# Halving the expert's unit of work in a fused one-core block stack, and moving elementwise work between GpSimd, ScalarE and VectorE

## Time and profile before

| | |
|---|---|
| runs, median of 3 | 3956.78 us (3954.4 to 3968.36) |
| the profiled execution, its own time | 3952.47 us |
| its span, first to last instruction | 3950.7 us |
| mean granted TensorE clock | 0.878 |
| TensorE busy | 3197.8 us (81%) |
| GpSimd busy | 3007.5 us (76%) |
| VectorE busy | 2802.2 us (71%) |
| ScalarE busy | 2373.0 us (60%) |
| DMA | 710.42 MB, mean 180 GB/s |

### The profile page before, as it was taken

One profiled execution on the slowest core, in us unless ns is written; L12 is line 12 of the kernel. 1 busy time (PEld: TensorE's weight loads), 2 busy tenths in 40 slices (PEclk: granted clock), 3 DMA queues, 4 the chain that ended last, 5 costly groups with the idle time before them and its releaser, 6 DMA issues. The chain is left out here.

```text
span 3950.7 us, 58606 instructions
## 1 busy us (share of the span) xinstructions
PE 3197.8 (81%) x17648; PEld 1963.8 (50%) x17648; DVE 2802.2 (71%) x5886; ACT 2373.0 (60%) x5235; POOL 3007.5 (76%) x2719
## 2 busy tenths in 40 slices
PE   5878787898879988798977988799877988769327
PEld 3545354564536654365544645366543655436105
DVE  3357878776886778677687677866787777877760
ACT  5566666666666656565676656666575656644321
POOL 1128888877888679786888778886898878898980
PEclk9888798899889998899888998799988998889558
DMA  2036777767687677776777676876777767797970
GB/s 67 6 90 180 207 181 197 207 162 211 173 211 189 164 213 183 199 188 191 193 193 199 173 209 164 218 192 166 215 186 195 188 190 200 184 245 208 242 179 32
DMA packets 406459, 710.42 MB, mean 180 GB/s; under 512 B 52922, under 2 KB 86338, under 8 KB 406146
## 3 DMA queue, kind: packets, MB, share of 16 engines
q1 hardware_dynamic: 406146, 706.68, 67.1%
HBM read 622.63 MB, written 83.89 MB: 179 GB/s over the span
## 5 line engine op out<-in xcount | busy, mean ns | idle before, releaser
L1417 POOL TENSOR_TENSOR u_rows<-u_rows,c_rows 128x512 f32<-128x512 f32 x1024 | 1340.4, 1310 | 325.9 <-DVE state L1227 255.5
L1410 POOL TENSOR_TENSOR u_rows<-u_rows,b_rows 128x512 f32<-128x512 f32 x1024 | 1348.3, 1318 | 14.6 <-DMA u_rows<-u_dram 14.1
L907 ACT ACTIVATE bank<-d_rows,a_rep 128x512 f32<-128x512 f32 x1024 | 693.4, 685 | 345.4 <-DMA d_rows<-delta_dram 148.0
L1222 DVE TENSOR_TENSOR_SCAN u_rows<-bank,state,u_rows 128x512 f32<-128x512 f32 x512 | 642.0, 1270 | 108.3 <-ACT bank L907 64.7
L1222 DVE TENSOR_TENSOR_SCAN u_rows<-bank,u_rows 128x512 f32<-128x512 f32 x512 | 622.6, 1216 | 108.1 <-ACT bank L907 99.7
L629 PE MATMUL bank<-u_rows,sum_n 128*32 128x512 f32 x2048 | 329.0, 719 | 357.2 <-POOL u_rows L1417 357.0
L749 ACT ACTIVATE prob<-prob,neg_max 128x256 f32<-128x256 f32 x1024 | 508.3, 501 | 83.9 <-DVE neg_max L1013 83.7
L1013 DVE CUSTOM_DVE_ANT_0 prob<-bank,band 128x256 f32<-128x256 f32 x896 | 337.0, 417 | 177.5 <-PE bank L460 141.7
L472 PE MATMUL bank<-ident,prob 128*128 128x128 f32 x2048 | 344.2, 298 | 115.6 <-ACT prob L749 55.5
L472 PEld LDWEIGHTS bank<-ident,prob 128*128 128x128 f32 x2048 | 256.7, 152 | 265.0 <-issue 173.6
L460 PE MATMUL bank<-kT,q_own 32*128 32x256 f32 x2048 | 317.5, 429 | 36.4 <-DVE neg_max L1013 26.2
(11 more groups left out here) (161 smaller groups left out, 5715.3 us busy)
## 6 DMA issues: line engine op xcount, KB each, us to landing
u_rows<-u_dram SPq DMA_DIRECT2D x1024, 256.0 KB, 5.0
d_rows<-delta_dram SPq DMA_DIRECT2D x1024, 256.0 KB, 5.0
zs_dram<-region_b SPq DMA_DIRECT2D x64, 256.0 KB, 2.7
xc_dram<-region_b SPq DMA_DIRECT2D x64, 256.0 KB, 2.6
delta_dram<-region_b SPq DMA_DIRECT2D x64, 256.0 KB, 2.1
u_dram<-region_b SPq DMA_DIRECT2D x64, 256.0 KB, 2.0
yg<-xc_dram SPq DMA_DIRECT2D x64, 256.0 KB, 3.3
zg<-zs_dram SPq DMA_DIRECT2D x64, 256.0 KB, 4.0
```

Of the source, the lines that this page charges most:

```text
L907: e.activation(banks[at.bank][:, :], delta_of(i, k), ACT.Exp, scale=a_rep[:, j:j + 1]).then_inc(filled[at.bank], 1)
L1222: e.tensor_tensor_scan(rows, banks[at.bank][:, :], rows, state[:, k:k + 1] if i % 2 else 0.0, ALU.mult, ALU.add).then_inc(drained[at.bank], 1)
L1410: e.tensor_tensor(rows, rows, b_rows[:, :], ALU.mult).then_inc(bx_ready.sem, 1)
L1417: e.tensor_tensor(rows, rows, c_rows[:, :], ALU.mult).then_inc(hc_ready.sem, 1)
```

## The change

1. `expert` is made for each group instead of each pair: 25 steps, 2 parts of 256 rows, between 0.44 and 0.97 of every period (group i in period i+4). A new stage `fetch` (0.39 to 0.40) loads the weights; for the second group of a pair it loads the two large ones once more, except for the last two pairs, where no MLP needs `w_1` and `w_2` in between. The MLP's weights are loaded back after each expert that still has an MLP to come.
2. GpSimd no longer forms `diff`, the squares or the epsilon sums. ScalarE makes `(1-mu)*x_prev` (four copies with a scale, from two new constants `not_mu_k` and `not_mu_r`); VectorE adds `mu*x` to it, makes the squares and the epsilon sums.
3. In scans 14 and 15 VectorE makes the product with B for the odd tiles, reading B from its PSUM bank, which stays taken until the last of them; GpSimd keeps the even tiles and all products with C.

```diff
@@ costs and threads
-    "route": [1] * 4,
-    "expert": [1] * 49,
+    "route": [1] * 3,
+    "fetch": [1],
+    "expert": [1] * 25,
...
-    (("route",), 3, 0.36, 0.40),
-    (("expert",), 3, 0.44, 0.97),
+    (("route",), 3, 0.36, 0.39),
+    (("fetch",), 4, 0.39, 0.40),
+    (("expert",), 4, 0.44, 0.97),
...
+def shared_inputs(i, batches):
+
+    return i >= 2 * batches - 2
...
-        return ([("b", 0, 1), ("c", 7, 8)]
+        return ([("b", 0, SCAN0 + 2 * (TILES - 1) + INPUT_AT if shared else 1), ("c", 7, 8)]
...
+        def fetched_again(i):
+
+            return i % 2 and i - 1 < 2 * BATCH - 4
@@ pe_mlp
-            if i % 2 == 0 and i >= 4:
-                e.wait_ge(*w_back.at(i // 2 - 2, 2))
+            if i >= 4:
+                e.wait_ge(*w_back.at(i - 4, 2))
@@ act_rwkv
             act_transposed(e, (use("t3.0"), use("t3.1")), norm_b)
             yield
+            e.wait_ge(*gone(use("t3.0")))
+            e.wait_ge(*gone(use("t3.1")))
+            for a, mu in ((1, "not_mu_k"), (0, "not_mu_r")):
+                for k in range(KD):
+                    e.activation(mixT[:, a, k, :], nb[:, k, 0:G], ACT.Copy, scale=col[mu][:, k:k + 1]).then_inc(mix_half.sem, 1)
@@ dve_stats
             e.wait_ge(*ln.stat.at(i, 3 * k + 2))
+            e.tensor_scalar(ln.rstd[:, :], ln.mean_var[:, :, 1], EPS, None, ALU.add)
@@ dve_rwkv
-            e.wait_ge(*diff_ready.at(i))
             for a, mu in ((1, "mu_k"), (0, "mu_r")):
                 for k in range(KD):
-                    e.scalar_tensor_tensor(out=mixT[:, a, k, :], in0=diff[:, k, :], scalar=col[mu][:, k:k + 1],
-                                           in1=nb[:, k, 0:G], op0=ALU.mult, op1=ALU.add).then_inc(mix_ready.sem, 1)
+                    e.wait_ge(*mix_half.at(i, 2 * (1 - a) + k + 1))
+                    e.scalar_tensor_tensor(out=mixT[:, a, k, :], in0=nb[:, k, 1:1 + G], scalar=col[mu][:, k:k + 1],
+                                           in1=mixT[:, a, k, :], op0=ALU.mult, op1=ALU.add).then_inc(mix_ready.sem, 1)
...
-            yield from range(8)
+            yield
+            for m in range(KD):
+                e.wait_ge(*gone(use(f"rk{m}")))
+                e.tensor_tensor(kT2[:, m, :], kT2[:, m, :], kT2[:, m, :], ALU.mult).then_inc(k_sq.sem, 1)
...
@@ dve_scan
+            def times_b(k):
+                at, rows = use("b"), rows_of(i, k)
...
+                e.wait_ge(*landed(u_landed, i * TILES + k))
+                ins = e.tensor_tensor(rows, rows, banks[at.bank][:, :], ALU.mult)
+                ins.then_inc(bx_by_vector.sem, 1)
...
             for step in range(SCAN_STEPS):
+                k = tile_at(step, INPUT_AT)
+                if k is not None and k % 2 and shared_inputs(i, BATCH):
+                    times_b(k)
@@ pool_rstd
-            e.tensor_scalar(ln.rstd[:, :], ln.mean_var[:, :, 1], EPS, None, ALU.add).then_inc(ln.power.sem, 1)
@@ pool_rwkv
-            e.tensor_tensor(diff, nb[:, :, 1:1 + G], nb[:, :, 0:G], ALU.subtract).then_inc(diff_ready.sem, 1)
...
-                e.tensor_tensor(kT2[:, m, :], kT2[:, m, :], kT2[:, m, :], ALU.mult).then_inc(k_sq.sem, 1)
@@ sp_fetch
+            if i % 2 == 0 or fetched_again(i):
+                e.wait_ge(*pick_ready.at(i // 2))
+                pick = e.value_load(top_i[0:1, 0:1], min_val=0, max_val=EXPERTS - 1)
+                e.wait_ge(*full(uses["mlp", min(i + 3, 2 * BATCH - 1), "m3"]))
+                if i:
+                    e.wait_ge(*gone(uses["expert", i - 1, "e1.5"]))
```

More of the change, by code:

```diff
@@ L132, in __init__, with banks_of @@
         self.bank, self.n, self.f = bank, n, f
[L135 removed]
+def banks_of(order, batches):
     begins, ends = {}, {}
     for stage in COSTS:
[L139 to L141 removed]
+        for shared in (False, True):
+            for name, first, last in uses_of(stage, shared):
+                begins.setdefault((stage, shared, first), []).append(name)
+                ends.setdefault((stage, shared, last), []).append(name)
     idle, counted, signalled, uses = list(range(8)), [0] * 8, [0] * 8, {}
     for stage, i, step in order:
[L144 removed]
+        shared = stage == "scan" and shared_inputs(i, batches)
+        for name in begins.get((stage, shared, step), ()):
             bank = idle.pop(0)
@@ L148, in banks_of @@
             signalled[bank] += not (stage == "scan" and name[0] == "y")
-        for name in ends.get((stage, step), ()):
+        for name in ends.get((stage, shared, step), ()):
             idle.append(uses[stage, i, name].bank)
```

188 lines of the change are left out of this document (96 added, 92 removed).

## The result

The changed kernel takes 3789.24 us, the median of 4 runs (3782.69 to 3797.62); the kernel before took 3957.41 in the same sessions (4 runs). The ratio is 0.9571, 95% interval 0.9544 to 0.9599: 168 us faster, where the forecast said 103. The profiled execution took 3792.8 us, its span is 3790.9, the mean granted clock 0.911 (0.878 before).

What follows compares the result with a forecast made beforehand. TensorE was taken to set the pace in periods with an expert, GpSimd or the attention and projection chain without. Six pairs -86, last scans -16, last product -1: -103, 3854 us; range 3785 to 3925, own range 3815 to 3895.

Steps and rivals of the forecast that it cites:

- TensorE per stretch with half an expert: Tiles 23 to 40: TensorE's work falls from 62.7 to 49.3 us at the high clock.
- Three engines stand near 50: Tiles 23 to 40: TensorE, GpSimd and VectorE near 50 us, none full; 54.5 us each period, -7.3 us a pair.
- The relief: GpSimd gives up 5.8 us a period; 4.0 counted inside the first stretch's 54.5, the rest -0.5 us a pair.
- Second stretch, 71.5 us in each period: Tiles 40 to 58: between the chain's 66.6 us and today's mean of 75.25; -7.5 us a pair.
- The terms of a pair together: Six scan pairs, each -7.3 and -7.5 for stretches, +1 weights, -0.5 GpSimd elsewhere: -86 us in all.
- Weights, +1 us a pair: Extra expert fetches and MLP weight reloads cost 1 us a pair, ends 0 and 10.4.
- Squares at 1.74 us, not 7.09: VectorE's two new squares per period priced at 1.74 us each, with 0.66 and 7.09 kept as extremes.
- Rival C: VectorE stands 7.09 instead of 1.74 us at both squares of every period: +128 us, 3982 us; chance 0.04.
- ScalarE's copies at nothing: Four new copies, 0.63 us each, 2.5 us a period, costed at nothing because ScalarE has idle time.
- The last two scans, -16 us: Scans 14 and 15: -7.5 and -8.5 us, with DMA and VectorE next to bound; ends -24 and nothing.
- D: Last two scans: DMA alone sets their pace, so +16 us, 3870 us; counted within the forecast's 0.76.
- Rival A, 3772 us: Both stretches with half an expert take today's expert-free 53.0 and 66.6 us; -185 us in all; chance 0.12.

Runs made afterwards that it cites:

- halves_alone: The kernel before with only the fetch stage and half experts added; 3891.40 us, ratio 0.9859 to the kernel before.
- no_refetch: The changed kernel without the second fetch of an expert's weights and the MLP reload between its halves; 3795.46 us, ratio 0.9593 to the kernel before.
- no_share: The changed kernel with all products with B left on GpSimd in scans 14 and 15; 3812.95 us, ratio 0.9637 to the kernel before.
- no_relief: The changed kernel with difference, squares and epsilon sums given back to GpSimd; 3852.40 us, ratio 0.9748 to the kernel before.
- squares_on_pool: The changed kernel with only the two squares of each period moved back to GpSimd; 3823.39 us, ratio 0.9670 to the kernel before.

## Why the forecast was right and where it was wrong

The direction was right, and the time lies inside the range, but only just: 4 us above its low end, with the lowest of the four runs (3782.69) below it. That it lies inside is in part luck, since the range had been drawn wide and steps failed in both directions. The size was not right: 103 us forecast, 168 measured. By its own steps:

- **TensorE per stretch with half an expert, "62.7 - 13.4 = 49.3 us at the high clock"**: right, 49.05 and 48.64 us, clock 1.00.
- **"Three engines stand near 50, in a fixed order, so none will be full: I take 54.5"**: this step failed. Tiles 23 to 40 took 49.8 and 49.2 us with TensorE busy 98 to 99% and GpSimd 99%. The forecast lost 5 us a stretch on an assumption without a row; the rows it had spoke against it, since the earlier trace rows show TensorE at 62.65 of 63.30 us in the same fixed order. The low end named for the two, -17.7 a pair, is what came in this pair: -17.3 (-15.0 in the mean of six). GpSimd was put at 45.9 us and was busy 49.2 and 48.7.
- **The relief "is inside the 54.5"**: wrong with it, and the larger miss. With half an expert and no relief the two stretches take 52.9 and 55.6 us (52.9 and 54.1 in `halves_alone`), so 54.5 was a fair price for the halves alone, and the relief came on top. By the ratios it is worth 70 us in all, against 3 us put down outside the first stretch and some part of 6 x 7.3 inside. It does not need the halves either: with whole experts it took 11.3 us off the pair of scans 8 and 9. The squares alone are 39 us. A detail was misplaced too: the difference of 1.89 us lies in tiles 8 to 23, where 3.0 us were gained in this pair and none forecast, and the first ten microseconds of gain came before scan 2, where there is no expert at all.
- **Second stretch, 71.5 us in each period**: right in the odd scan (72.5), 10 us off in the even one (81.7). The step that failed is the path: for both kinds of period the forecast took "the 66.6 that the chain takes without any expert" as all that lies under TensorE. The 66.6 us of the earlier trace rows are an odd scan's, and in an even scan a second chain, through VectorE's edge ops, is longer: the halves alone reached 76.6 us, and the held edge op added 5. "TensorE sets the pace", read from 76.6 of 83.9 us busy at clock 0.98, was true before the change. The forecast compared this stretch with the one without an expert and took all that differed for the expert. The middle stage of an odd group differed as well. The pair became 3.7 us longer, inside the end of +5 that was given.
- **The terms of a pair together**: in this pair 11.2 us less came than forecast in the second stretch, 10.0 more in the first, and 3.0 and 3.7 in tiles 8 to 23 and behind tile 58, which were costed at nothing. So 86 against 108.1 looks better than its terms are.
- **Weights, +1 us a pair**: too high if anything; `no_refetch` is not faster than the change, though 6 us in all lie at the edge of what these runs can tell.
- **Squares at 1.74 us, not 7.09**: right, median 1.30, largest 1.71. Rival C is out. The hold exists nevertheless, and struck elsewhere: it left the residual for an edge op. The statement that it ends when GpSimd runs out of released work held in all 77 cases.
- **Product with B from PSUM at 0.675 us**: right, 656 to 690 ns while GpSimd streams.
- **ScalarE's copies at nothing**: nothing in the traces speaks against it; the whole relief, with them, gained about what GpSimd was relieved of.
- **The last two scans, -16 us**: too small, -41.5. In scan 14 the prices 41.5, 48 and 56 us met 40.1, 41.4 and 57.7; the middle one failed, since VectorE was busy 41.0 us there and not 46.6. In scan 15 "the DMA share makes floors of 35.2, 39.4 and 41.3" failed: measured 34.3, 35.4 and 37.4. The share times the length of the stretches changed little (115.9 us before, 113.5 now); what failed is the silent assumption that the share ends at 1. It reads 1.06 at up to 269 GB/s. There both engines now wait for the transfers, as D had it, only at a lower time. VectorE and GpSimd waiting for them in scan 15, where the earlier trace rows showed VectorE waiting for GpSimd:

```profile
DVE u_rows L1288 <- DMA u_rows<-u_dram: 24.9, 20, 3.3
```

```profile
POOL u_rows L1448 <- DMA u_rows<-u_dram: 16.7, 21, 2.8
```

Not all of this is the shared inputs: `no_share` takes 181.0 and 158.1 us for the two scans, the change 173.1 and 135.1. So sharing is worth 31 us there by the traces (26 by the ratios), and the other 10.7 of scan 14's gain come from the first two parts. In scan 15 they bring nothing: 158.0 before, 158.1 without sharing.
- **Rival A, 3772 us**, came nearest in time and is half right in its reason: the first stretch absorbed everything (49.5 against its 53.0), the even second one nothing (81.7 against 66.6), and what was gained before scan 2 and in the last scans, more than A had there, made up for a part of it. The time came out 17 us above A's and 65 under the forecast's, and neither had the reason.

What stays open: why the hold picks one instruction and not its neighbour. `no_relief`, `no_share`, `squares_on_pool` and the change place it differently with nearly the same instructions, and no run here steers it. So no run separates by design how much of the edge ops' 53 us is the hold and how much the ops with their waits in turn. By periods with and without a hold in `no_share` and `no_refetch` (80.6 to 82.6 us against 77.0 to 79.0), and 73.0 in the mean without the ops, some 4 us a period are the hold and 5 the ops. Why the state copies cost more on ScalarE is open too.

## What to carry to other kernels

Cut the time into stretches with the same work and compare neighbours for all that differs, not only for the part you mean to move: a stretch can have two bounds near one height, and then removing the first gains only the distance to the second, or nothing. Where an engine is close behind the one that sets the pace, as GpSimd was here, price its relief in every stretch, and look for elementwise work to take off it. A DMA share below or near 1 while another engine sets the pace is no floor.
